# Value product of the last batch's attention: from one float32 matmul to three fp32r matmuls on split operands

## The reference

```python
kv_input = jnp.concatenate([xn, ln], axis=1)      # 1601 + 512 = 2113 keys
k, v = jnp.split(kv_input @ Wkv, 2, axis=-1)      # 16 heads of 64
w = softmax(einsum('bhqd,bhkd->bhqk', q * scale, k * scale), axis=-1)
out = einsum('bhqk,bhkd->bhqd', w, v)             # then @ Wout
```

## Time and profile before

| what | us |
|---|---|
| median of 3 runs (3147.78 to 3148.49) | 3148.29 |
| the profiled execution, its own time | 3144.86 |
| its span in the trace | 3143.1 |
| PE busy in the span | 2954.3 |
| ACT busy | 1343.6 |
| DVE busy | 1973.0 |
| POOL busy | 1070.3 |

### The profile page before, as it was taken

The page is one execution under the profiler, slowest core; times in us unless marked ns, Lnnn a source line. Parts: engine busy times, 40 slices in busy tenths (PEclk is TensorE's granted clock), DMA queues, the critical chain, the costliest instruction groups (busy, mean ns, idle before and its releaser), DMA issues. The chain is left out here.

```text
span 3143.1 us, 33934 instructions
## 1 busy us (share of the span) xinstructions
PE 2954.3 (94%) x11590; PEld 1850.7 (59%) x11590; DVE 1973.0 (63%) x3403; ACT 1343.6 (43%) x2309; POOL 1070.3 (34%) x838
## 2 busy tenths in 40 slices
PE   7576899999999999999999999999999999899996
PEld 3233566656665656565656566666656565676666
DVE  5897677775658777666777776665555554452225
ACT  4642454454455454536454544354343434211121
POOL 3196466662006676600376664000000000102213
PEclk9788899999999999999999999999999999899998
DMA  5341221121121111211221212101010100411112
GB/s 218 150 163 68 74 71 58 34 65 55 38 68 58 35 58 35 71 35 38 75 58 35 71 50 63 38 15 40 19 38 15 38 15 14 168 57 53 51 44 69
DMA packets 71679, 189.84 MB, mean 60 GB/s; under 512 B 8420, under 2 KB 39272, under 8 KB 63448
## 3 DMA queue, kind: packets, MB, share of 16 engines
q1 hardware_dynamic: 67096, 172.08, 18.0%
q0 software_dynamic: 3984, 15.60, 1.5%
q10 hardware_dynamic: 432, 0.01, 0.0%
HBM read 124.59 MB, written 28.44 MB: 49 GB/s over the span
## 5 line engine op out<-in xcount | busy, mean ns | idle before, releaser
L987 ACT ACTIVATE a_carry<-a_st 128x512 f32<-128x512 f32 (+1 forms) x1088 | 649.1, 597 | 1126.7 <-PE a_st L1368 1118.7
L1380 PE MATMUL a_o<-a_carry,a_vals 128*65 128x512 f32 (+1 forms) x2176 | 1113.7, 593 | 0.0
L1145 DVE TENSOR_REDUCE a_maxes<-a_mx 128x1 f32<-128x512 f32 x1024 | 683.0, 686 | 220.0 <-PE a_mx L1296 213.3
L1368 PE MATMUL a_st<-a_q,a_kone 65*128 65x512 f32 (+1 forms) x1088 | 431.5, 397 | 0.0
L884 POOL TENSOR_TENSOR a_shared<-a_shared,a_bc 128x512 f32<-128x512 f32 x192 | 251.5, 1310 | 384.9 <-DVE a_shared L1083 384.9
L1380 PEld LDWEIGHTS a_o<-a_carry,a_vals 128*65 128x65 f32 (+1 forms) x2176 | 284.1, 137 | 103.5 <-issue 1.8
L1367 PE MATMUL a_st<-a_q,a_keven 128*128 128x512 f32 (+1 forms) x544 | 325.9, 599 | 0.7 <-issue 0.7
L855 POOL TENSOR_TENSOR a_erstd<-a_emv,a_half 128x4 f32<-128x4 f32 x8 | 8.1, 1014 | 906.9 <-DVE a_emv L1171 906.9
L1367 PE MATMUL a_st<-a_q,a_kodd 128*128 128x512 f32 (+1 forms) x544 | 314.9, 579 | 0.0
L1296 PE MATMUL a_mx<-a_kodd,a_q 128*128 128x512 f32 x512 | 298.4, 599 | 7.2 <-DVE a_maxes L1145 6.1
L1083 DVE TENSOR_TENSOR_SCAN a_shared<-a_shared 128x512 f32<-128x512 f32 x192 | 288.6, 1505 | 12.7 <-POOL a_shared L873 11.6
(11 more groups left out here) (251 smaller groups left out, 4404.9 us busy)
## 6 DMA issues: line engine op xcount, KB each, us to landing
a_bc<-m_kept_bc SPq DMA_DIRECT2D x48, 512.0 KB, 3.7
a_wt<-a_w_split SPq DMA_DIRECT2D x15, 1536.0 KB, 9.5
a_kone<-a_keven SPq DMA_DIRECT2D x32, 528.5 KB, 4.5
a_kone<-a_kodd SPq DMA_DIRECT2D x32, 528.5 KB, 4.2
e_wall<-in_w_t_dram SPq DMA_DIRECT2D x27, 512.0 KB, 9.6
a_early<-m_kept_bc SPq DMA_DIRECT2D x16, 512.0 KB, 3.7
a_w_split<-a_wt POOLq DMA_DIRECT2D x4, 1536.0 KB, 5.5
a_shared<-in_ctx_dram SPq DMA_DIRECT2D x4, 1536.0 KB
```

Source lines behind the costliest of these rows:

```text
L987: nc.scalar.activation(p_of(s % 4)[0:r], st[0:r, s % 2], ACT.Exp, scale=SCALE).then_inc(exp_done, 1)
L1145: nc.vector.reduce_max(maxes[:, c, t:t + 1], mx[:, i % 2], AX_X).then_inc(mx_max, 1)
L1368: nc.tensor.matmul(st[0:r, s % 2], k_one[g % 2][0:DH + 1, kt * P:kt * P + r], qm[of(g)][0:DH + 1, :], start=False, stop=True).then_inc(st_ ...
L1380: nc.tensor.matmul(ps_o[0:DH + 1, g % 2], vals[0:r, kt * HG + j, :], p_of(s % 4)[0:r], start=(kt == 0), stop=(kt == KT - 1)).then_inc(pv_d ...
```

## The change

For the last batch (`g >= SPLIT_HEAD = 48`) both operands of the value product are split into a fp32r high part and a fp32r low part (the remainder), and the product becomes three fp32r matmuls: high x high, low values x high exponentials (64 columns, without the ones), high values x low exponentials. The term low x low is left out.

- ScalarE: after each exponential it waits for its own write and copies it to `p_high` (fp32r). It also makes the high parts of the values from the ring bank (`high`, kind "V").
- GpSimd: `low_exp(s)` subtracts `p_high` from the exponential into `p_low`. `exp(s)` waits in addition for `low_exp(s - 4)`, which reads the buffer that it writes.
- VectorE: for the values of the last batch, the copy becomes a subtraction (bank minus high part), which waits for ScalarE's high part before it frees the bank.
- TensorE: `add_o` waits for the high part, issues two matmuls, waits for the low part and issues the third.
- The new buffers lie over memory whose data is no longer needed then (`carry`, `y`, `bc_gate` with part of `shared`, `vals`).

```diff
+SPLIT_HEAD = (B - 1) * H
+SPLIT_GROUP = SPLIT_HEAD // HG
+HIGH = {x: i for i, x in enumerate(x for x in MADE if x[0] in "QK" or x[0] == "V" and x[1] >= SPLIT_GROUP)}
...
+            def low_exp(s):
+                r = tile_rows(s % KT)
+                pool.wait_ge(p_high_ready, s - SPLIT_HEAD * KT + 1)
+                nc.gpsimd.tensor_tensor(p_low(s)[0:r], p_of(s % 4)[0:r], p_high(s)[0:r].bitcast(F32),
+                                        ALU.subtract).then_inc(p_low_ready, 1)
...
+                    if g >= SPLIT_HEAD:
+                        low_exp(g * KT + kt)
...
+                else:
+                    t, w = VB[i]
+                    r = tile_rows(t)
+                    act.wait_ge(pv_done, (n * HG - 1) * KT + t + w)
+                    if n == SPLIT_GROUP:
+                        nc.scalar.activation(vals_high[0:r, t * HG:(t + w) * HG, DH:DH + 1],
+                                             vals[0:r, t * HG:(t + w) * HG, DH:DH + 1], ACT.Copy)
+                    a = nc.scalar.activation(vals_high[0:r, t * HG:(t + w) * HG, 0:DH],
+                                             ring[0:r, k, 0:w * GW].rearrange("p (a d) -> p a d", d=DH), ACT.Copy)
...
+                if s >= SPLIT_HEAD * KT + 4:
+                    act.wait_ge(p_low_ready, s - SPLIT_HEAD * KT - 3)
                 nc.scalar.activation(p_of(s % 4)[0:r], st[0:r, s % 2], ACT.Exp, scale=SCALE).then_inc(exp_done, 1)
+                if s >= SPLIT_HEAD * KT:
+                    act.wait_ge(exp_done, s + 1)
+                    nc.scalar.activation(p_high(s)[0:r], p_of(s % 4)[0:r], ACT.Copy).then_inc(p_high_ready, 1)
...
-                    o = nc.vector.tensor_copy(vals[0:r, t * HG:(t + w) * HG, 0:DH], made)
+                    if n >= SPLIT_GROUP:
+                        o = nc.vector.tensor_tensor(vals_low[0:r, t * HG:(t + w) * HG], made,
+                                                    vals_high[0:r, t * HG:(t + w) * HG, 0:DH].bitcast(F32),
+                                                    ALU.subtract)
+                    else:
+                        o = nc.vector.tensor_copy(vals[0:r, t * HG:(t + w) * HG, 0:DH], made)
...
+                if g >= SPLIT_HEAD:
+                    high, low = vals_high[0:r, kt * HG + j, :], vals_low[0:r, kt * HG + j]
+                    pe.wait_ge(p_high_ready, s - SPLIT_HEAD * KT + 1)
+                    nc.tensor.matmul(ps_o[0:DH + 1, g % 2], high, p_high(s)[0:r], start=(kt == 0), stop=False)
+                    nc.tensor.matmul(ps_o[0:DH, g % 2], low, p_high(s)[0:r], start=False, stop=False)
+                    pe.wait_ge(p_low_ready, s - SPLIT_HEAD * KT + 1)
+                    nc.tensor.matmul(ps_o[0:DH + 1, g % 2], high, p_low(s)[0:r], start=False, stop=(kt == KT - 1)).then_inc(pv_done, 1)
+                    return
```

More of the change, by code:

```diff
@@ L569 @@
 AT = {x: i for i, x in enumerate(x for x in MADE if x[0] in "QKVOTP")}
-HIGH = {x: i for i, x in enumerate(x for x in MADE if x[0] in "QK")}
+SPLIT_HEAD = (B - 1) * H
+SPLIT_GROUP = SPLIT_HEAD // HG
+HIGH = {x: i for i, x in enumerate(x for x in MADE if x[0] in "QK" or x[0] == "V" and x[1] >= SPLIT_GROUP)}
 POW = {x: i for i, x in enumerate(x for x in MADE if x[0] in "EGL" or x[0] == "A" and x[2] == 1)}
@@ L582, in sem @@
             return ctx.enter_context(nc.semaphore(name))
+        with ExitStack() as later:
+            p_high_all = later.enter_context(nc.sbuf_tensor("a_phigh", [P, 2, CT, S], F32R))
+        p_high = lambda s: p_high_all[:, s % 4 // 2, s % 2]
         carry = sb("a_carry", [P, 2, CT, S])
         y = sb("a_y", [P, CT, S])
+        with ExitStack() as later:
+            p_low_all = later.enter_context(nc.sbuf_tensor("a_plow", [P, CT, S], F32R))
+        p_low = lambda s: p_low_all[:, s % 4]
         bc_gate = sb("a_bc", [P, CT, S])
+        with ExitStack() as later:
+            vals_low = later.enter_context(nc.sbuf_tensor("a_valslow", [P, KT * HG, DH], F32R))
         shared = sb("a_shared", [P, CTX_T * DM + 2 * TT * DM])
@@ L617, in attention @@
         early = sb("a_early", [P, 6 * S + 2 * KVP + 32])
+        with ExitStack() as later:
+            vals_high = later.enter_context(nc.sbuf_tensor("a_valshigh", [P, KT * HG, DH + 1], F32R))
         vals = sb("a_vals", [P, KT * HG, DH + 1])
@@ L657, in attention @@
         exp_done = sem("a_exp_done")
+        p_high_ready = sem("a_p_high_ready")
+        p_low_ready = sem("a_p_low_ready")
         pv_done = sem("a_pv_done")
```

## The result

The change makes the kernel faster by 1.0%: 3115.16 us at the median against 3148.03 (the kernel before, with a fourth run), ratio 0.9897 with a 95% interval of 0.9885 to 0.9909. The forecast was 3113 us.

What follows compares the result with a forecast made beforehand. TensorE's stream was taken to bound the last batch: 43.0 us gained, less 1.7 (head 63), 5 (odd heads) and 1 (value pieces), saves 35.3, giving 3113 us; forecast 3107 to 3118, stated range 3101 to 3128.

Steps and rivals of the forecast that it cites:

- TensorE's part: Value product in the last batch: three fp32r matmuls replace the float32 product, saving 0.158 us a step, 43.0 us over 272.
- the tail: End of the batch: last low part comes 3.2 us after the last scores, against 3.44 TensorE needs; nothing gained or lost.
- Rival (d): Value product on TensorE: float32 costs what four passes cost, in some hidden way, giving 3092 us; chance 0.03.
- ScalarE's pair: Exponential plus its new copy on ScalarE, each step: 1.25 us, up to 1.35; not the bound over a head, with exceptions.
- head 63: Last head, bare steps: TensorE needs 1.17 us, ACT 1.25 to 1.35; thirteen steps lose 1.0 to 2.4 us, taken as 1.7.
- The start of odd heads: Query and key splitting: copies delay ScalarE, so TensorE finds the bank full; seven heads lose 2.5 to 6.6 us, taken 5.
- rival (b): Last batch's 15 full heads: ACT and POOL bind more often, losing a further 0.5 to 1.5 us each; 3120 to 3136; chance 0.16.
- The value pieces: 40 pieces in four groups: an added ACT copy frees the bank some 0.8 us later; loss 0 to 2 us, taken 1.
- POOL: GpSimd's subtraction, each last-batch step: about 1.3 us, 22 us of a 26.4 us head; latency covered; level with TensorE in head 63.
- rival (c): GpSimd's subtraction in the last batch takes 2.2 us and becomes the bound: about +59 us, 3207; chance 0.07.
- The sum: Whole kernel: 43.0 - 1.7 - 5 - 1 = 35.3 us saved, giving 3113 us at the median (-1.1%).

Runs made afterwards that it cites:

- The two orderings: Against the changed kernel, DVE's reductions of maxima go ahead of its subtractions in the last batch: everywhere 3118.60 us; except in steps with an output piece 3104.59 us.
- the freed ScalarE: Against the changed kernel, the copy of the exponential moves from ScalarE to POOL, which then makes both parts: 3154.74 us in one run.

## Why the prediction was right

- **TensorE's part** was right in kind and 4% too small: 0.165 us a step and not 0.158, seen in more than 200 steps; over the 269 value products that lie within the stretch, 44.4 us. The forecast counted all 272 at the full saving and the tail as neither gained nor lost, which can't both be: the last three lie in the tail. Rival (d), four passes priced at the distance of fp32r matmuls (0.234 saved a step), is out.
- **ScalarE's pair** was over-priced. I took 1.25 to 1.35 us from a row in which the copy starts 0.11 us after its predecessor ends. Here it starts 0.03 after it, and the next exponential 0.54 after that: 2640.89, 2641.49, 2642.03, the pair in 1.14 to 1.15 us, just under TensorE's step. So head 63 lost nothing where I had put 1.7 us.

```profile
2640.89 0.58 ACT L1023 ACTIVATE a_carry<-a_st 128x512 f32<-128x512 f32 x1
2641.49 0.63 ACT L1026 ACTIVATE a_phigh<-a_carry 128x512 fp32r<-128x512 f32 x1
2642.03 0.58 ACT L1023 ACTIVATE a_carry<-a_st 128x512 f32<-128x512 f32 x1
```

- **The start of odd heads** cost 1.1 us a head, 7.9 in all, against my 5 and outside its bounds (2.5 to 6.6): this term of the sum was mis-sized. The bank of the queries in step 2 was the named mechanism and cost 0.4 a head. The larger part, 1.0 in step 4, is a link that my sum left out and only rival (b) touched: the reductions queue behind the key's subtraction on DVE. The two orderings and the freed ScalarE show both halves of it.
- **The value pieces** cost 4.1 us against my 1 (0 to 2), 0.5 of it in head 47: not the ring's banks, as I argued, but the same queue on DVE.
- **POOL** took 1.29 us a subtraction and 1.25 from start to start (nine in 11.29 us), as forecast, and its latency is covered in the steps. In head 63 it was not level with TensorE, as I had it, but slower, and the tail lost 0.3 us by it where I had put nothing. No subtraction was above 1.351 us in the trace, so rival (c) did not occur; moving the copy onto POOL showed that its price was about right: at 1.84 to 1.91 us a step nearly all of the gain is gone. The Trainium skill (SBUF — State Buffer, Who interferes with whom) says that a DVE instruction with at most one SBUF input, outside the modes that use two ports (which `tensor_scalar` can enter), does not contend with GpSimd; the 272 subtractions agree, with DVE busy for half of the stretch. Four `tensor_scalar` instructions with input and output in SBUF stand in the last batch, at the end of head 48, and there DVE paid: they take 1.38 us each beside POOL's subtractions and 0.40 before the change.

```profile
2160.84 5.29 DVE L1220 TENSOR_SCALAR rows<-rows,a_emv,a_erstd 128x256 f32<-128x256 f32 x4
```

  Before, the four took 1.37 us together (2157.39). Head 49 is no longer for it than the other heads of its kind (35.38 against 35.32 to 35.40 us).
- **The sum** came out near because the terms erred against each other. Gained were 44.4 us instead of 43.0, and lost 7.9 + 4.1 + 0.3 = 12.3 instead of 7.7, which leaves 32.1, against 35.3 forecast and 32.9 measured between the medians. Step by step it is 32.6 for the last batch, less 0.5 in head 47 and 0.3 in the tail, 31.8. That the forecast of 3113 lies 2 us from the median is in part luck: ScalarE's 1.7 us in head 63, which did not come, made up for part of what odd heads and value pieces cost beyond their bounds. By kind of head: 2.8 and 2.4 us saved in g % 4 == 2 and 0 (2.5 to 2.8 forecast; head 48 only 1.6), 1.7 and 1.0 in odd heads (1.7 to 2.3), 2.8 in head 63 (0.5 to 1.8).

## What to carry to other kernels

When the bounding engine gets faster by about a tenth of a step, look first at the steps where two helpers hand a buffer on one after the other; there the slack goes first, and it goes through whatever is queued behind the waiting instruction of the second helper. An instruction that waits for a third engine belongs behind those whose data is ready, unless a buffer that it frees is needed at once: the same reordering won 1.0 us in one step and lost 1.5 to 1.7 in another. Compare such traces step by step from the starts of one instruction; the totals by engine show none of this.

## What was not expected of the hardware

A ScalarE copy that waits for ScalarE's own write of 128x512 started 0.03 us after that write's end, all 272 times, against 0.11 us behind instructions of 128x256. An instruction without such a wait starts about 0.09 us before its predecessor ends (2642.03 against 2642.12 in the rows of ScalarE above), so the wait itself costs some 0.12 us.

TensorE's granted clock fell to its lower level in two of the experiments, once each, after idle times of TensorE of 1.41 and 1.05 us, and that cost a head 1.6 and 3 us. Other idle times about as long, in the same traces, left it at 1.00, so what decides it is open. In the changed kernel it stayed at 1.00 through the last batch.

And the first stage, whose code no version changed, ended up to 4.3 us earlier or later from one trace to the next (its first value product at 350.9 to 355.2 us), more than several of the effects measured here.
